# Masked attention scores written back in place into PSUM, without SBUF tiles for them and without the wait between two maxima

## The reference

```
q, k = split(x @ W_attn + b_attn); v = x (per head)
y    = causal_attention(q, k, v)
e    = v[1:] - y[:-1];  k2 = x[:-1] @ W_k2 + b_k2
y2   = causal_attention(q[1:], k2, e)
x    = layernorm(x + proj(y) + proj(y2))
x    = layernorm(x + expert_ffn(x))      # experts: the first 512 rows only, zero for the rest
```

## Time and profile before

| | |
|---|---|
| median of 3 runs | 2493.94 us (2493.41 to 2496.92) |
| the profiled execution, its own time | 2490.87 us |
| its span, first to last instruction | 2488.8 us |
| mean granted TensorE clock | 0.995 |
| DMA, mean | 101 GB/s |

### The profile page before, as it was taken

One profiled execution on the slowest core, in us unless ns is written; L12 is line 12 of the kernel. 1 busy time (PEld: TensorE's weight loads), 2 busy tenths in 40 slices (PEclk: granted clock), 3 DMA queues, 4 the chain that ended last, 5 costly groups with the idle time before them and its releaser, 6 DMA issues.

```text
span 2488.8 us, 64954 instructions
## 1 busy us (share of the span) xinstructions
PE 2380.8 (96%) x19670; PEld 1308.3 (53%) x19670; DVE 2122.8 (85%) x9275; ACT 1772.9 (71%) x3392; POOL 1506.0 (61%) x2342
## 2 busy tenths in 40 slices
PE   6999999999999999999999999999999999999996
PEld 4555555555555555555555555555555555555454
DVE  5888889888898988888898888888988888998655
ACT  3677777777777777777777777777777777777752
POOL 4466666666666666666666666666666666665432
PEclk9999999999999999999999999999999999999998
DMA  6555555555655556565555656555555555555121
GB/s 117 94 102 105 98 105 100 99 111 108 116 106 98 98 97 115 107 117 108 101 98 94 114 107 112 109 100 101 97 107 109 109 113 105 100 100 88 55 66 45
DMA packets 187732, 250.82 MB, mean 101 GB/s; under 512 B 26744, under 2 KB 103168, under 8 KB 187392
## 3 DMA queue, kind: packets, MB, share of 16 engines
q1 hardware_dynamic: 186432, 245.10, 53.1%
q10 hardware_dynamic: 960, 1.57, 0.5%
HBM read 74.60 MB, written 16.78 MB: 37 GB/s over the span
## 4 chain that ended last, share of the span: by engine, by line
PE 74%; ACT 11%; issue 6%; POOL 4%; DVE 3%; DMA 1%; ACTq 0%; SPq 0%; DVEq 0%; POOLq 0%
PE out_t L631 22%; PE score_t L670 19%; PE misc L723 12%; PE score L681 7%; PE misc L766 5%; ACT heads_t L555 5%; PE out_t L696 5%; ACT prob L529 4%; DVE junk L889 2%; PE score L825 1%; POOL prob L437 1%; PE misc L750 1%; ACT part_f L541 1%; PE score L841 1%; ACT resid L276 1%
## 5 line engine op out<-in xcount | busy, mean ns | idle before, releaser
L889 DVE CUSTOM_DVE_ANT_0 junk<-score,mask_rows 128x384 bf16<-128x384 f32 (+3 forms) x3584 | 1689.2, 515 | 256.9 <-PE score L681 237.3
L529 ACT ACTIVATE prob<-score_t 128x512 f32<-128x512 f32 x2560 | 1367.9, 599 | 447.5 <-PE score_t L670 446.5
L437 POOL TENSOR_SCALAR_AFFINE_SELECT prob<-prob 128x512 f32<-128x512 f32 (+1 forms) x1280 | 711.3, 559 | 829.7 <-ACT prob L529 829.5
L670 PE MATMUL score_t<-stack_q,stack_k 50*128 50x128 f32 (+5 forms) x4096 | 995.1, 359 | 21.9 <-ACT prob L529 6.9
L681 PE MATMUL score<-stack_k,stack_q 48*128 48x512 f32 (+3 forms) x4096 | 987.2, 348 | 2.9 <-DVE max_cols L889 1.8
L670 PEld LDWEIGHTS score_t<-stack_q,stack_k 50*128 50x128 f32 (+1 forms) x4096 | 610.8, 186 | 570.9 <-ACT prob L529 308.5
L631 PE MATMUL out_t<-prob,value 128*17 128x512 f32 (+3 forms) x8192 | 668.1, 437 | 1.0 <-POOL prob L437 0.7
L681 PEld LDWEIGHTS score<-stack_k,stack_q 48*128 48x128 f32 x4096 | 616.2, 188 | 24.2 <-DVE max_cols L889 12.7
L889 DVE DVE_READ_ACCUMULATOR2_ANT max_cols<- 128x1 f32 x4096 | 338.7, 83 | 0.0
L631 PEld LDWEIGHTS out_t<-prob,value 128*17 128x17 f32 x8192 | 187.8, 97 | 273.1 <-issue 209.1
L459 POOL TENSOR_TENSOR part_l<-part_f,part_h 128x512 fp32r<-128x512 f32 x192 | 254.3, 1325 | 16.2
(11 more groups left out here) (99 smaller groups left out, 1716.4 us busy)
## 6 DMA issues: line engine op xcount, KB each, us to landing
stack_k<-part_h SPq DMA_DIRECT2D x512, 128.0 KB, 4.3
stack_k<-part_l SPq DMA_DIRECT2D x256, 128.0 KB, 5.1
stack_q<-part_h SPq DMA_DIRECT2D x248, 128.0 KB, 4.2
x_full<-x_turned SPq DMA_DIRECT2D x32, 512.0 KB, 12.1
x_in<-L_attn_x SPq DMA_DIRECT2D x32, 512.0 KB, 13.7
resid<-L_attn_x SPq DMA_DIRECT2D x32, 512.0 KB, 5.4
stack_q<-part_l SPq DMA_DIRECT2D x124, 128.0 KB, 5.1
layer_out<-resid SPq DMA_DIRECT2D x31, 512.0 KB, 6.6
```

The costliest lines, as they stand in the source:

```text
L437: e.affine_select(out=view, in_=view, compare_op=ALU.is_ge, fill=0.0, base=-unit_parts(unit)[1], pattern=[[0, runs], [0, cut], [1, P]], ch ...
L529: e.activation(prob[pair % RING][:, slot % 2 * 512:slot % 2 * 512 + 512], score_t[time % KEY_DEPTH][:, :], ACT.Exp, scale=1.0 / np.sqrt(HE ...
L670: done = e.matmul(score_t[now % KEY_DEPTH][:, col:col + n], keys[rows, pair, kb * P:(kb + 1) * P], stack_q[b % 2][rows, pair, kb * P:token ...
L889: e.tensor_tensor_reduce(junk[count % JUNK][:, 0:n], score[number % MAX_DEPTH][:, col:col + n], mask, 1.0, -3e38, ALU.add, ALU.max, max_co ...
```

## The change

The two `junk` tiles and the wait on the call two before are gone. The pass over the columns now writes the masked scores as f32 over the scores that it reads, in their own columns of their own PSUM bank. The waits on `s_qry` (a bank is full) and, on TensorE's side, on `s_max` (a bank is free) stay. The next matmul into the bank overwrites what lies there.

```
-RING, KEY_DEPTH, MAX_DEPTH, JUNK = 6, 3, 3, 2
+RING, KEY_DEPTH, MAX_DEPTH = 6, 3, 3
...
-        junk = [sb(f"junk{i}", [P, tokens], BF16) for i in range(JUNK)]
...
                         if i == 0:
                             e.wait_ge(s_qry, number + 1)
-                        if count >= JUNK:
-                            e.wait_ge(s_max, count - JUNK + 1)
-                        e.tensor_tensor_reduce(junk[count % JUNK][:, 0:n], score[number % MAX_DEPTH][:, col:col + n], mask, 1.0, -3e38,
+                        scores = score[number % MAX_DEPTH][:, col:col + n]
+                        e.tensor_tensor_reduce(scores, scores, mask, 1.0, -3e38,
                                                ALU.add, ALU.max, max_cols[b % 2][:, a, head % SIDES, head // SIDES, qb:qb + 1]).then_inc(s_max, 1)
```

## The result

The changed kernel takes 2531.29 us (median of 4 runs, 2529.69 to 2535.72) where the kernel before takes 2493.68 us: 37.6 us more, ratio 1.0153 (1.014 to 1.0167). I had forecast 2493.5 us, and a range that ended at 2515. The profiled execution has a span of 2530.5 us against 2488.8.

A forecast was written before the change was run, and what follows sets the result against it. TensorE was taken to bound the kernel. From the 2493.94 us median, 0.1 us came off for the wait, nothing for tiles or PSUM write, and a few tenths for other late steps: 2493.5 us, range 2482 to 2515.

The forecast's parts named there:

- That TensorE bounds the steady state and VectorE comes second: Over one 72 us batch, TensorE was taken as busy 70.11 us and VectorE 63.90 us.
- elsewhere the chain runs over TensorE's matmuls: Outside two passages through VectorE in a batch, the chain was said to follow TensorE's matmuls and ScalarE's copy of `out_t`.
- The wait: Removed wait on the call two before: 0.02 us late behind 128-column calls, 512 times; worth 0 to 10 us, taken as 0.1.
- places 3 and 7: Points in each batch where `neg_l` and the residual stand in VectorE's queue and the last-ending chain passes through VectorE.
- x = 0: Change in one masked-maximum call's step from writing to PSUM: taken as zero, bounded by -78 and +77 ns.
- The signal: At the read-out of a maximum: its signal may come later by 25 to 50 ns, behind a longer write.
- Rival 2: The PSUM write costs 25 to 50 ns a call, or delays the read-out's signal as much: 2500 to 2515 us; chance 0.12.
- a longer "issue" before TensorE goes on: Profile sign of a small write cost: the 0.14 us between a maximum's read-out and TensorE's start, before 1039.13, would grow.
- 222 calls on the path: Calls whose step reaches the end: 192 at two passages a batch and 30 in the lead-in; 2.2 us for 10 ns.
- Rival 1: One PSUM bank as source and destination loses the overlap between passes, 77 ns for each of 4096 calls: about 2550 us; chance 0.09.
- stretches of 9 us: Eight parts of a batch; VectorE's busy time plus 1.0 us a unit exceeded 9 us by 2.3 us a batch.
- The Trainium skill's rule: VectorE takes 58 cycles beside the columns from SBUF, 120 from PSUM: estimated 65 ns for a PSUM operand, weighed but not used.

The follow-up runs named there:

- the bench: VectorE alone, nothing of the layer computed: ten calls in a row of each kind; a 512-column masked maximum steps 611 ns into SBUF, 649 ns into PSUM.

## Why the prediction was wrong

**That TensorE bounds the steady state and VectorE comes second** held, and so did the period, but "elsewhere the chain runs over TensorE's matmuls" was read as "elsewhere there is room". The chain names VectorE only where TensorE has already stopped. It doesn't say how near the others are. At slot 2 TensorE had no room in seven of eight units: 172 ns of a later signal became 0.17 us of lag.

**The wait: right in its bounds.** Worth 0 to 10 us, taken at 0.1: the batch is 0.02 us shorter without it (72.05 us), and 0.03 us shorter, not longer, with it back in the changed kernel (73.13). The run without it leaves a gain of 1 to 6.5 us by its interval, so 0.1 may have been too little. The chain of before does name line 888 once at each of places 3 and 7, 0.02 us, behind a call of 512 columns, where I had looked behind the short ones alone:

```profile
1037.63 0.02 DVEq L888
```

**x = 0: the first step that failed.** It was +38 ns for each pass that starts with a read-out, some 2900 of 4096. It lay inside my bounds of -78 and +77 ns, but the rows I took as nearest (425 ns from PSUM, 421 ns from SBUF) differ in a source, and the change moves a destination. Nor did I consider the pair: line 889 is two instructions with two destinations, and the change parted them. The row for the clearing of `out_t` was right in what it said, that a write into PSUM isn't slow in itself; plain adds cost nothing.

**The signal: a term mis-sized.** Rival 2 allowed the read-out's signal to come later "by as much" as x. It came 58 ns later on top of the 38. Its sign, a longer "issue" before TensorE goes on, did not come: that is 0.14 us in both chains, because the delay lies in the read-out itself, 141 ns instead of 83.

**222 calls on the path: the second step that failed.** Rival 2 with x = 38 ns gives 222 x 38 = 8.4 us; 37.6 us were measured. The count took two passages a batch, with three calls each. There are one or two waits in almost every unit: for four calls of 256 in a row (172 ns late) and for the last of slot 4 (2 x 38 + 58 = 134 ns late), and at both TensorE was already following. The row that pointed there was in the waits of before, 515 times "issue" in front of the weight loads of `score_t`. That isn't two for each of 256 units: 154 of them at slot 2 and 96 at slot 7 stand 0.12 us behind the end of a read-out. Taken from the timeline instead, whatever the profile puts the wait down to, slot 2's weight load stands that 0.12 us behind the last read-out of slot 9 in seven of eight units, in the kernel before as after.

**Rival 1** had the mechanism of a lost overlap wrong (a following pass still starts before the one before has ended, 0.38 us apart with a duration of 0.47), though its range of 2533 to 2567 us begins only 2 us above the result. Its working by stretches of 9 us, applied to x = 38 ns, gives 16 x 0.038 = 0.61 us for a unit, so 9.45, 9.16 and 9.46 us in three of the eight stretches, an excess of 1.07 us a batch: the measured 1.09 us. This agreement is luck: not all 16 passes of a unit pay, and the lag enters in seven units and not in three stretches.

**The Trainium skill's rule** on PSUM operands, 58 against 120 cycles in "VectorE: DVE Perf Modes", section "The TRN2 errata", isn't what was seen: in the bench a source in PSUM and one in SBUF give 611 and 612 ns into SBUF. Its estimate of 65 ns would have been nearer than my zero, for a reason that these runs don't bear out. The same page's section "Two Vector instructions with no wait between them" counts an accumulator's read-out as an instruction of its own and holds an instruction only where start quadrants differ within one memory. All tiles here start at partition 0, so by that rule nothing is held. The trace agrees in that the next pass still starts with the read-out (18.91 us in the bench); the 38 ns come all the same, and the rule has no price for them.

**The ends of the run.** The lead-in of the changed kernel shows a clock of 0.55 from 30 to 66 us, the lower of the two levels (1.2 GHz) from 33.8 us on; TensorE was busy 2.5 of the 3.6 us before that fall, and the kernel before, busy 2.6 of 3.0 us there, kept 2.4 GHz. The kernel with both writes in PSUM has the same clock there and reaches its first transposition at 64.4 us, as before (64.1 us) does:

```profile
30.00:66.00 36.00, 32.30 (x85) 19.06 (x85) 29.96 (x137) 5.78 (x5) 9.28 (x10) 0.55 0.79 121
```

Its third transposition is at 135.7 us, against 135.1 before and 138.1 after. So the clock explains at most 0.5 of the lead-in's 3.0 us, and the rest goes with VectorE's calls. Why the clock fell isn't known. The 4 us of the last stretch stay open too: it took 153.8 us in that same kernel, and the clock differs between executions there.

## What to carry to other kernels

A VectorE instruction with an accumulator output has two destinations; keep them in one memory, or pay 38 ns for each call that follows another without a pause, and a signal 58 ns later. When a second engine gets slower by tens of ns, don't count the places where the chain already passes through it; find every wait for it, and how long after its signal the waiting engine's next weight load starts: if that gap is the same each time (0.12 us here), the engine already follows, and there is no margin: 172, 97 and 76 ns of a later signal became lags of 0.17, 0.09 to 0.10 and 0.07 us. A wait that has long been met may be left standing: taking it away measured 0.15%, and the write that replaced its tiles cost ten times that.

## What the runs showed of the hardware

The step of a masked maximum is 611 ns at 512 columns with pass and read-out in one memory, SBUF or PSUM, and 649 ns with them in two, with the same 38 ns at 128 and 256 columns. A pass pays them only where it starts with the read-out of a call with two memories and writes where the pass before wrote; behind an idle of VectorE its step stays (350 ns at 256 columns in the layer). At 512 columns the read-out lasts 82 to 91 ns with one memory and 141 ns with two. Reading and writing one PSUM bank in one instruction costs nothing over writing another (649 and 649 ns). Plain adds have a step of 598 ns wherever they write, alternately too. On ScalarE a copy from PSUM keeps its step of 477 ns into SBUF and into PSUM, and its duration in the profile grows from 640 to 737 ns.
